# VectorE's order at the end of a pass: the first statistics of the next batch ahead of the second residual

## The reference

```
h = layernorm(x)
for l in range(4):
    xn = ln(h, ln1_w[l], ln1_b[l])               # first norm: mean and variance of each token
    q, k, v = xn @ Wq.T + bq, xn @ Wk.T + bk, xn @ Wv.T + bv     # 16 heads of 8
    scores = (q @ k.T + rel_shift((q + u) @ r.T)) * 8 ** -0.5    # causal
    h = h + softmax(scores) @ v @ Wo.T + bo      # first residual
    fn = ln(h, ln2_w[l], ln2_b[l])               # second norm
    h = h + gelu(fn @ W1.T + b1) @ W2.T + b2     # second residual
x = x + h
out = x + experts(layernorm(x))
```

## Time and profile before

| | |
|---|---|
| median of 3 runs | 2311.6 us (2310.13 to 2312.68) |
| the profiled execution: its own time | 2312.34 us |
| its span, first to last instruction | 2310.4 us |
| granted TensorE clock, mean | 0.991 |
| TensorE matmul busy | 2206.6 us, 96% of the span |
| TensorE weight load busy | 1900.8 us, 82% |
| VectorE busy | 1894.9 us, 82% |
| ScalarE busy | 1846.8 us, 80% |
| GpSimd busy | 1233.4 us, 53% |

### The profile page before, as it was taken

One profiled execution on the slowest core, in us unless ns is written; L12 is line 12 of the kernel. 1 busy time (PEld: TensorE's weight loads), 2 busy tenths in 40 slices (PEclk: granted clock), 3 DMA queues, 4 the chain that ended last, 5 costly groups with the idle time before them and its releaser, 6 DMA issues. The chain is left out here.

```text
span 2310.4 us, 81563 instructions
## 1 busy us (share of the span) xinstructions
PE 2206.6 (96%) x30592; PEld 1900.8 (82%) x30592; DVE 1894.9 (82%) x4687; ACT 1846.8 (80%) x2741; POOL 1233.4 (53%) x2217
## 2 busy tenths in 40 slices
PE   4899999999999999999999999999999999799998
PEld 3788888888888888888888888888888888688887
DVE  6788888888888888888888888888878886577774
ACT  3688888888888888888888888888878888656554
POOL 4555666655655555556555556565555554333332
PEclk8999999999999999999999999999999999999999
DMA  5444443433344343344434434433444342111100
GB/s 136 125 123 131 124 113 107 111 107 110 109 112 117 107 111 107 108 111 111 111 109 112 111 108 110 112 108 106 113 120 113 107 111 82 31 29 29 28 24 19
DMA packets 268388, 229.55 MB, mean 99 GB/s; under 512 B 37216, under 2 KB 266720, under 8 KB 268000
## 3 DMA queue, kind: packets, MB, share of 16 engines
q1 hardware_dynamic: 268000, 224.32, 35.2%
HBM read 14.46 MB, written 4.19 MB: 8 GB/s over the span
## 5 line engine op out<-in xcount | busy, mean ns | idle before, releaser
L985 DVE TENSOR_REDUCE rowmax<-bank 128x4 f32<-128x1024 f32 (+1 forms) x768 | 908.9, 1215 | 90.1 <-PE bank L582 87.7
L802 ACT ACTIVATE probs<-bank 128x1024 f32<-128x1024 f32 x768 | 737.6, 1024 | 124.0 <-PE bank L641 112.8
L641 PE MATMUL bank<-qstack,kstack 64*128 64x128 f32 (+1 forms) x4096 | 424.5, 300 | 14.7 <-DMA qstack<-maxrows 14.7
L582 PE MATMUL bank<-kstack,qstack 62*128 62x256 f32 (+1 forms) x4096 | 416.7, 301 | 6.5 <-DMA qstack<-base_turned 6.5
L641 PEld LDWEIGHTS bank<-qstack,kstack 64*128 64x128 f32 x4096 | 316.7, 192 | 17.2 <-DMA qstack<-maxrows 17.2
L582 PEld LDWEIGHTS bank<-kstack,qstack 62*128 62x128 f32 x4096 | 316.1, 193 | 6.9 <-issue 6.9
L1148 POOL CAST xn1T_parts<-xn1T 128x256 fp32r<-128x256 f32 x128 | 50.9, 397 | 460.1 <-ACT xn1T L810 460.1
L714 PE MATMUL bank<-w,hidden 128*128 128x128 f32 x2048 | 285.4, 283 | 3.3 <-ACT hidden L850 2.8
L604 PE MATMUL bank<-maskT_half,pick_half 64*128 64x128 bf16 (+1 forms) x3072 | 269.6, 241 | 15.2 <-ACT probs L802 5.4
L661 PE MATMUL bank<-probs,v_pad 128*32 128x256 f32 x4096 | 271.0, 382 | 0.6 <-DVE v_tok L966 0.6
L544 PE MATMUL bank<-mask_half,pick_half 64*128 64x128 bf16 (+1 forms) x3072 | 268.3, 242 | 2.1 <-DVE rowmax L985 0.9
(11 more groups left out here) (149 smaller groups left out, 5099.5 us busy)
## 6 DMA issues: line engine op xcount, KB each, us to landing
qstack<-base SPq DMA_DIRECT2D x384, 128.0 KB, 2.5
kstack<-base SPq DMA_DIRECT2D x384, 128.0 KB, 2.6
qstack<-base_turned SPq DMA_DIRECT2D x384, 128.0 KB, 2.4
turn_x<-turn_c SPq DMA_DIRECT2D x512, 32.0 KB, 1.8
ctx_den<-ctxT_raw SPq DMA_DIRECT2D x256, 64.0 KB, 2.0
ctx_num<-ctxT_raw SPq DMA_DIRECT2D x256, 64.0 KB, 2.0
qstack<-maxrows SPq DMA_DIRECT2D x256, 16.0 KB
out<-ot SPq DMA_DIRECT2D x16, 256.0 KB, 2.4
```

The costliest lines, as they stand in the source:

```text
L582: last = pe.matmul(bank[:, b0 + b, i * wide:(i + 1) * wide], qstack[rows, r, p0 + i, t * 128:(t + 1) * 128], kstack[rows, r, p0 + i, 0:wid ...
L641: last = pe.matmul(bank[:, b0 + b, i * wide:(i + 1) * wide], kstack[rows, r, p0 + i, kt * 128:(kt + 1) * 128], qstack[rows, r, p0 + i, q0: ...
L802: act.activation(probs[:, k], bank[:, A_BANK[k]:A_BANK[k] + 2, :], ACT.Exp, scale=SCALE).then_inc(exp_done[k], 1)
L985: dve.tensor_reduce(rowmax[:, n % 2, t, :, p0:p0 + heads], bank[:, M_BANK[k]:M_BANK[k] + 2, :].rearrange("p b (h c) -> p b h c", h=heads), ...
```

## The change

On VectorE, `stats_1` leaves the head of the pass and goes between `maxrows_out` and `resid_2`, one pass earlier; `stats_1(0)` is put ahead of the loop. As the head of pass `s + 1` follows the end of pass `s` at once, the only two steps that change places are `resid_2(s - 6)` and `stats_1(s + 2)`: the statistics are now taken ahead of the residual. Both exist in passes 6 to 125, that is 120 times. No instruction is added or removed, and no other queue is touched.

```
                 dve.tensor_tensor(h, bank[:, DOWN_BANK, 0:S], h, ALU.add).then_inc(h2_ready, 1)
 
+            stats_1(0)
             for s in SLOTS:
-                if live(s + 1):
-                    stats_1(s + 1)
                 if s == -1:
                     clear_stack(3)
                 if live(s - 2):
...
                     apply_2(s - 5)
                 if live(s - 2):
                     maxrows_out(s - 2)
+                if live(s + 2):
+                    stats_1(s + 2)
                 if live(s - 6):
                     resid_2(s - 6)
                 if s == N + 3:
```

## The result

The median of six runs is 2295.27 us (2288.04 to 2296.36) against 2312.11 us for the kernel before (2309.77 to 2313.72): ratio 0.9921, 95% interval 0.9909 to 0.9933, which is 16.8 us. The forecast was 2288.6 us; it is 6.7 us too low and its range holds the result. The profiled execution is the fastest of the six, 2288.04 us with a span of 2286.1 us, 24.3 us under the profiled one of before.

The account below looks back on a forecast made before the run. TensorE sets the pace, held up once a pass by VectorE's row maxima ahead of `f2`. 100 x 0.23 = 23.0 us off 2312.34 gives 2289.3 us, less 0.7 us for the median: 2288.6 us, range 2279 to 2302 us.

Parts of the forecast that it names:

- The chain: VectorE from the end of `down`: `resid_2`, `stats_1`, maxima of rounds 2 and 1, then `f2`; every piece counts, `stats_1` 0.68 us.
- They fit into the wait for `down`: Behind `maxrows_out` on VectorE: statistics fit the 0.77 us idle time with 0.09 us to spare; `resid_2` doesn't move.
- 0.23 us a pass: Ahead of `f2`: maxima, and so `f2`, start 0.23 us earlier each pass; bounds 0.14 and 0.31 us.
- pass 127: Pass with no unit left for `stats_1`: maxima start 0.44 us after round 2's products start, taken as their new place.
- 100 passes: Passes that gain: 113 with `f2`'s wait for row maxima, less 13 where a5 waits for the maxima's transfers.
- The median: Whole kernel: the median of the runs was put 0.7 us below the profiled execution, giving 2288.6 us from 2289.3 us.
- the rival in which transfers eat the gain: Round a5 on TensorE: more waits for transfers take the gain from every third gaining pass, leaving 15.3 us, 2296.3 us; 10%.
- No change: Round a2 on TensorE: its wait for the exponential replaces the removed one; gain 0 to 4 us, 2310 us; 7%.
- slower: Masks of round m1 wait for a `resid_2` over 0.59 us late; 2324 us for the first 0.1 us beyond; 2%.
- The lock between VectorE and GpSimd: Moved statistics hold up GpSimd's split of `xn1T` by 0.68 us; a5 waits, 7 us gain left, 2304.6 us; 3%.

Follow-up runs that it names:

- experiment 3: Kernel before with two more `bn_stats` per unit, into an unread tile, ahead of the statistics at the head of the pass: 2355.11 us, ratio 1.0183.
- experiments 2 and 6: Kernel before, first statistics left out from unit 8 on: 2292.22 us; kernel before, first statistics put between the maxima of rounds 1 and 4: 2292.49 us.
- experiment 8: Changed kernel with SyncE's queue issuing the two transfers of the maxima ahead of the three of the turned base: 2283.35 us, ratio 0.9885.
- experiment 5: Changed kernel with four more `bn_stats` ahead of the moved statistics: 2297.80 us, ratio 0.9939.
- experiment 1: The changed kernel run again, unaltered: 2294.28 us, ratio 0.9922.

## Why the prediction was right, and where its size was off

**The chain.** Right. VectorE's order from the residual to `f2` was serial (experiment 3 pays 0.40 us for 0.39 us), and taking the statistics out of it gives the whole gain (experiments 2 and 6 can't be told from the change).

**They fit into the wait for `down`.** Right: 1.18 us from `maxrows_out` to the residual, before and after. They had more room than the 0.09 us I reckoned: they start 0.34 us behind the start of `maxrows_out`, at 1017.19, not at its end 0.41 us behind it.

**0.23 us a pass.** This term was mis-sized: it measured 14.91 - 14.72 = 0.19 us in the median pass, 0.21 us in the one shown. Over 100 passes that is 4 of the 6.2 us by which the gain fell short of 23.0 us. The start of the maxima did move as read from pass 127, 0.44 us behind the products (1018.82 - 1018.38). But from there to `f2`'s weights it is 1021.29 - 1018.82 = 2.47 us, not the 2.44 us I had carried over. The second reduction starts 1.14 us behind the first where the first had waited (1019.96 - 1018.82), and in tow it was 1.11 us; a row of the kernel before, from a narrow window, shows its start beside the 1028.40 of the earlier trace rows:

```profile
1029.51 2.41 DVE L985 TENSOR_REDUCE rowmax<-bank 128x8 f32<-128x1024 f32 x2
```

**100 passes.** The count is borne out: unit by unit from 6 to 126, comparing each profile of before with each of the changed kernel, 88 to 96 of 121 passes are 0.15 to 0.25 us shorter, and a pass in which TensorE waits elsewhere can gain nothing, as the pair of single passes in experiment 8 shows. 100 x 0.19 = 19.0 us is within 2.2 us of the 16.8 us measured. a5 and a2 wait 1.9 us more on average, which would account for it, but this isn't shown to the microsecond. Those waits vary by 1 us between two profiles of one kernel, the falls of the clock by 1.5 us, the start of unit 6's `f2` by 3 us in the profiles of these two kernels, and medians of the kernel before in four sets of runs by 3.5 us. In the two profiles on each side these 121 passes together are 21.5 us shorter on average, more than the medians differ by. So the 2.2 us stay open.

**The median.** I took the profiled execution's offset of 0.7 us over. It cannot be seen in one profile that the changed kernel's own executions lie over 8 us, from 2288.0 to 2296.4 us.

**The rivals.** By the number alone, the rival in which transfers eat the gain (2296.3 us) came closer to 2295.27 us than my forecast did. Its mechanism doesn't fit: it left the pass at 0.23 us and took every third gain away, but the median pass gained 0.19 us, a5 waits in 12 and 16 passes against 13 and 11 before, and a5 and a2 together took 2 of some 19 us, not a third. No change and slower: no; experiment 5 puts the residual 0.60 us late, and TensorE loses 0.06 us a pass. The lock between VectorE and GpSimd: no. GpSimd's two splits, the first wholly beside the moved statistics (1017.19 to 1017.94), last what they lasted, 0.40 and 0.74 us:

```profile
1017.31 0.40 POOL L1149 CAST xn1T_parts<-xn1T 128x256 fp32r<-128x256 f32 x1 [3.43 <-ACT xn1T L810]
1017.79 0.74 POOL L1151 TENSOR_TENSOR xn1T_parts<-xn1T,xn1T_parts 128x256 fp32r<-128x256 f32 x1
```

By the rule of the Trainium skill ("SBUF — State Buffer", Who interferes with whom) an instruction with at most one SBUF input, outside the two-port modes, does not contend with GpSimd. The trace agrees, by the same 0.40 and 0.74 us.

**Not tried.** What would free the last 0.14 us ahead of `f2`, whether fewer or larger transfers end the hold-ups in SyncE's queue, and what a kernel without the falls of the clock in units 8, 14 and 113 would give.

## What to carry to other kernels

Follow the waits of the busiest engine back through the other engine's order, and move out of that stretch whatever nobody in it needs; here it made no difference whether it went into idle time ahead of the chain or behind what `f2` waits for. Look in the trace for a place where the moved piece is missing, here the first pass without a next unit: it gave the new start of the maxima to the hundredth. Count the gain only in the passes where that wait ends last, since a wait that is removed had also been taking up other delays, and those now cost their full length. And look at the granted clock of a long pass before its length is put down to waits.

## What the runs showed of the hardware

- An instruction of VectorE that follows another at once (in tow) took less time than one that had to wait: the next reduction started 1.11 us behind it against 1.14 us, and the residual was 0.39 us long, with 0.30 us to the next start, against 0.42 and 0.34 us. Two `bn_stats` in tow took 0.39 us to the next start, four 0.78 us (experiment 5), while the record of two shows 0.48 us.
- SyncE's queue is held up now and again: three issues in 3.32 us where 1.83 us is usual. Where the hold-up falls decides whether anyone waits. In the same profile one of the six transfers of `base` took 1.80 us in place of 0.60 us (at 1447.10 us), and no wait of a5 follows in the next pass; ahead of the maxima it cost 0.65 us.
- TensorE's granted clock fell from 1.00 to 0.50 (2.4 to 1.2 GHz) for some microseconds once in a pass with a long wait: in unit 113 of experiment 1 at the end of 3.87 us of idling, in unit 113 of the kernel before some 1.5 us after TensorE had gone on from 3.48 us of idling. The wait of 2.98 us in the changed kernel's first profile was followed by no fall. A fall cost 1.6 to 1.9 us or 2.5 to 3.3 us beyond the wait.
